# Attention on one core: the products with the values moved directly behind the scores

## The reference

```python
q = (hidden_states @ wq.T + bq) * scaling          # 12 heads of 16 columns
k = hidden_states @ wk.T + bk
v = hidden_states @ wv.T + bv
k = p_rope(k, positions); q = p_rope(q, positions)
attn = jnp.einsum('bqd,bkd->bqk', q, k)
attn = jax.nn.softmax(attn, axis=-1)
out = jnp.einsum('bqk,bkd->bqd', attn, v)
...
return out @ wo.T + bo
```

## The kernel before

| round | between scores and turn_heads | behind turn_heads and values |
|---|---|---|
| 0 | | turn_x1 (L941), first part |
| 1 (opens with turn_max L928 and turn_x1, second part) | | project_qk, first half (L948) |
| 2 | turn_back, first half (L972) | project_qk, second half (L948) |
| 3 | turn_back, second half, turn_xq | project_v (L948) |
| 4 | turn_o (L851, L853) | |
| 5 (opens with project_o L859, L862) | | feed_forward |

## Time and profile before

### The profile page before, as it was taken

The page is one execution under the profiler, slowest core; times in us unless marked ns, Lnnn a source line. Parts: engine busy times, 40 slices in busy tenths (PEclk is TensorE's granted clock), DMA queues, the critical chain, the costliest instruction groups (busy, mean ns, idle before and its releaser), DMA issues.

```text
span 1587.4 us, 36344 instructions
## 1 busy us (share of the span) xinstructions
PE 1507.7 (95%) x11313; PEld 1233.0 (78%) x11313; DVE 1347.7 (85%) x3200; ACT 1240.4 (78%) x2686; POOL 849.9 (54%) x1400
## 2 busy tenths in 40 slices
PE   4889999999999999999999998999999999999986
PEld 3678888888888888888888886677777777777763
DVE  5789999999999999999999886677888878888764
ACT  4678878798888888888888964777887877787873
POOL 7888844543334343333333236566666666666642
PEclk9899999999999999999999997999999999999996
DMA  5633200010000000000000000000000000000000
GB/s 111 149 51 76 37 1 34 1 34 0 0 1 1 1 1 0 0 1 1 1 1 0 1 1 1 2 8 12 12 11 15 11 11 11 11 11 15 11 12 26
DMA packets 24445, 27.14 MB, mean 17 GB/s; under 512 B 3105, under 2 KB 22433, under 8 KB 24353
## 3 DMA queue, kind: packets, MB, share of 16 engines
q1 hardware_dynamic: 16672, 19.70, 3.8%
q0 software_dynamic: 7680, 6.30, 3.2%
HBM read 14.58 MB, written 6.29 MB: 13 GB/s over the span
## 4 chain that ended last, share of the span: by engine, by line
PE 49%; DVE 20%; ACT 13%; issue 12%; POOL 4%; DVEq 1%; DMA 0%; ACTq 0%; POOLq 0%
PE banks L948 7%; PE banks L916 6%; PE banks L873 5%; PE banks L900 5%; PE banks L731 5%; DVE x L1579 4%; PE banks L887 4%; PE banks L722 4%; DVE xs L1481 3%; DVE hs_h L1542 3%; ACT xs L1205 3%; ACT ht L1195 2%; PE banks L859 2%; PE banks L972 2%; PE banks L862 2%
## 5 line engine op out<-in xcount | busy, mean ns | idle before, releaser
L1646 DVE TENSOR_REDUCE mx<-banks 128x4 f32<-128x1024 f32 x192 | 234.2, 1220 | 45.7 <-PE banks L887 45.2
L1254 ACT ACTIVATE probs<-banks 128x1024 f32<-128x1024 f32 x192 | 195.8, 1020 | 83.5 <-PE banks L900 80.3
L520 POOL TENSOR_TENSOR x<-x,bo_row 128x768 f32<-128x768 f32 (+1 forms) x64 | 121.3, 1896 | 144.2 <-DVE ucr_r L1507 144.2
L722 PE MATMUL banks<-ht,w_uv 128*128 128x512 f32 x576 | 169.4, 403 | 16.5 <-ACT sv_l L1228 14.7
L496 POOL TENSOR_TENSOR lnt<-mv,const 128x4 f32<-128x4 f32 x64 | 28.2, 441 | 270.2 <-DVE mv L1472 270.2
L1498 DVE SCALAR_TENSOR_TENSOR uc_h<-u_h,vec,uc_h 128x512 f32<-128x512 f32 x192 | 149.0, 776 | 1.8 <-ACT uc_h L1166 1.8
L722 PEld LDWEIGHTS banks<-ht,w_uv 128*128 128x128 f32 x576 | 110.1, 194 | 45.3 <-issue 13.9
L1481 DVE SCALAR_TENSOR_TENSOR xs<-x,rstd,xs 128x192 fp32r<-128x192 f32 x256 | 90.0, 413 | 41.3 <-ACT xs L1205 41.3
L722 PE MATMUL banks<-ht,w_uv_rest 128*128 128x512 f32 x384 | 121.7, 399 | 0.0
L900 PE MATMUL banks<-q_t,k_t 64*128 64x256 f32 x768 | 108.7, 334 | 7.8 <-ACT probs L1254 6.3
L1145 ACT ACTIVATE u_l<-banks,vec 64x256 f32<-64x256 f32 x128 | 60.0, 469 | 67.5 <-PE banks L722 66.7
(11 more groups left out here) (189 smaller groups left out, 4706.4 us busy)
## 6 DMA issues: line engine op xcount, KB each, us to landing
out_dram<-y_out SPq DMA_DIRECT2D x32, 192.0 KB, 2.0
x<-pos SPq DMA_DIRECT2D x12, 384.0 KB, 4.3
raw_z<-w_z_dram SPq DMA_DIRECT2D x4, 704.0 KB, 5.5
raw_uv<-w_uv_dram SPq DMA_DIRECT2D x4, 576.0 KB, 3.9
q_t<-mx_t SPq DMA_DIRECT2D x64, 6.0 KB
emb<-w_qkv_dram SPq DMA_DIRECT2D x1, 864.0 KB, 7.0
w_o<-w_o_dram SPq DMA_DIRECT2D x1, 768.0 KB, 5.3
x<-embedding_dram,idx POOLq DMA_INDIRECT x48, 4.4
```

Source lines behind the costliest of these rows:

```text
L722: last = nc.tensor.matmul(out[:], w, r[:], start=(k == 0), stop=(k == len(passes) - 1))
L1254: act.activation(probs[:, (s + g // 2) % 2, g % 2, :].rearrange("p (j k) -> p j k", j=2), B_SST, ACT.Exp, scale=float(DH) ** -0.5).then_in ...
L1646: nc.vector.tensor_reduce(mx[:, s].rearrange("p t (j h) -> p j t h", j=2)[:, :, :, g], B_SS.rearrange("p j (t k) -> p j t k", t=2), AX, AL ...
```

## The change

In TensorE's list of a step, the call of `values` (with the `emptied` for `xt_saved` that guards its bank in round 0) moves from behind `turn_heads` to directly behind `scores`, ahead of `turn_back` (round 2), `turn_o` (round 4) and `turn_heads` (rounds 0, 2, 4). Nothing is added or removed, and no other engine's list changes.

```diff
                     scores(at(3) if g == 0 else at(2), (g - 1) % 6)
 
+                    if g == 0 and not last:
+                        emptied(at, 8, xt_saved, 1, 1)
+                    if g % 2 == 0:
+                        values(at(5) if g == 0 else at(4), (g // 2 - 1) % 3)
+
                     if g == 2:
                         emptied(at, 2, tr_saved, 6, 2)
                         turn_back(at(5), 0)
...
                     emptied(at, *((3, tr_saved, 6, 6), (1, h1_ready, 2, 1), (1, qk_saved, 2, 1), (1, qk_saved, 2, 2),
                                   (1, v_saved, 1, 1), (2, tr_saved, 6, 5))[g])
                     turn_heads(at(2), g)
-                    if g == 0 and not last:
-                        emptied(at, 8, xt_saved, 1, 1)
-                    if g % 2 == 0:
-                        values(at(5) if g == 0 else at(4), (g // 2 - 1) % 3)
-
                     if g == 0:
                         if not ending:
                             emptied(at, 8, y_ready, 1, 1)
```

## The result

The changed kernel takes 1648.72 us (median of 4 runs, 1646.57 to 1651.93) against 1588.95 us (4 runs): a ratio of 1.038, interval 1.036 to 1.040. It is slower by 60 us. The prediction was 1636, range 1611 to 1650: the direction and the mechanism hold. The time lies 13 us above the value, near the upper end of the range, and 4 us above the 1645 that the prediction's own upper bounds add up to. The profiled execution took 1646.57 us with a span of 1644.4, 57.0 more than before.

A forecast was written before the change was run, and what follows sets the result against it. TensorE's list was taken as the bound. Per full step 0.51 + 0.50 + 0.62 - 0.07 = 1.56 us, over 28 steps 43.7, plus 2.3 for the last steps, on 1589.7, gives 1636 us; range 1611 to 1650.

The forecast's parts named there:

- upper bounds: Upper sizes of the three round delays, 0.60, 0.57 and 0.68 us, 1.85 a step, giving 1645 us.
- TensorE's list is the bound: Attention stage: TensorE busy 18.14 of 18.30 us a step, so nothing idle makes up for waits the reordering opens.
- Round 0, +0.51: Later heads delay ScalarE's `save_heads`, `save_o`, `save_x1`, and so `turn_heads` 1 and `project_qk`, by 0.51 us a step.
- Round 2, +0.50: The second half of `project_qk` waits for VectorE's `o_rows`, with only `turn_heads` as cover: 0.50 us a step.
- Round 4, +0.62: ScalarE's `turned` to `exps` 5 start 1.00 us later, delaying the next `scores_t` 0 by 0.62; `project_o`'s 0.39 is contained.
- Given back, -0.07: The wait before `scores` 5 in round 0 for VectorE's maxima falls inside the new one, saving 0.07 us a step.
- A full step: The three round delays less the part given back: 1.56 us a step, 43.7 us over 28 steps.
- The last steps, +2.3: Steps m = 33 to 35: 3 x 0.6 us where `turn_o` and `exps` meet, plus 0.5 for round 0 of m = 33.
- Rival 4: New gaps lower the clock; a tenth of the stage at half clock adds 25 us, giving 1661; chance 0.05.
- Weight loads, 0: Fewer borders between `values` and full-width work count 0, because TensorE waits for another engine at all three places.
- Rival 2: Faster by hidden weight loads, 0.17 us in round 0, up to 0.27 in rounds 2 and 4: 1570; chance 0.07.
- Rivals 1 and 3: Rival 1: only round 4's delay arrives, 1609, chance 0.13. Rival 3: waits cancel what the borders give back, 1590, chance 0.05.

The follow-up runs named there:

- single moves: Three kernels, `values` moved ahead in round 0, 2 or 4 only, against the kernel before: 1600.81, 1605.27 and 1607.61 us against 1586.09.
- a kernel of its own: New order only from m = 33 on, old order in the steps up to m = 32, against the kernel before: 1599.07 us against 1586.89.
- the third group in round 1: Kernel before, with `values` of `at(5)` moved from round 0 behind `turn_heads` 1, and `save_o` to ScalarE's round 1: 1619.41 us against 1586.89.
- the one with `values` in between: Kernel before, with `values` in rounds 2 and 4 put behind `turn_back` or `turn_o` but ahead of `turn_heads`: 1587.83 us against 1586.09.
- full steps only: New order only up to m = 32, old order in the last six steps, against the kernel before: 1632.38 us against 1586.89.

## Why the prediction was right, and where it was off

The full steps came out as worked out, and they are 44 of the 60 us. That the total lies inside the range is partly luck: the last steps cost 10 us more than they were given, the measured time is above the 1645 of the upper bounds, and it is inside only because the range was drawn 5 us wider than they allow.

- **TensorE's list is the bound, and nothing idle makes up for a wait.** Right: the busy time in the full steps is unchanged to 0.4 us, and the idle time grew by 43.9 of the 44.4 us.
- **Round 0, +0.51.** Measured alone +0.48. The path was as told, through `save_heads`, `save_o`, `save_x1` to `turn_heads` 1. The wait in front of `turn_max` was 0.41, not 0.2 to 0.3, inside the same sum as said.
- **Round 2, +0.50.** +0.56, with `project_qk` behind o_rows in all steps. Its start, 1235.83, lies 0.71 us behind the end of `turn_back`, against the 0.66 of the work on VectorE plus 0.06 to 0.13 for the signal.
- **Round 4, +0.62.** +0.58, on the path as told. `project_o` waits 0.54 us for or_t; its first matmul starts 0.82 us behind the end of `turn_o` (1.31 before, in the same timeline), with the 1.00 of `values` 0.51 later, where I had 0.39. `scores_t` 0 starts 4.08 us behind the end of `turn_o` (4.52 before), so 0.56 later, where I had 0.62. Its matmuls wait for `exps` 5 in 14 of 20 steps, not in every one.
- **Given back, -0.07.** Not borne out. The wait of the loads of `scores` 5 for VectorE's maxima, 3.5 us in 22 steps before, should have gone inside the new one; it is still 2.8 us in 20 steps, 0.14 a step instead of 0.16. Without the term the sum is 1.63, where 1.58 was measured. The single moves sum to 1.62; where the 0.04 between them and the whole goes is not shown.
- **A full step.** 1.56 predicted, 1.58 measured; 28 of them 43.7 and 44.4 us.
- **The last steps, +2.3: the term that was mis-sized.** It measured 12.3 in the profiled execution, and 12.2 in the median time of a kernel of its own. About 3 us are the replies, as priced. The rest is the clock. Rival 4 had put its fall in the full steps, where gaps of 0.5 us did not touch it (1.00 throughout), at a chance of 0.05, and not in the last steps, where TensorE is busy only 71% (45.9 of 64.7 us) before the change and the clock already falls in part of the stretch. The row for that stood in the page (the last digit of its PEclk row is 6); I priced the waits there and not the clock. That a clock can fall inside full steps, as rival 4 has it, shows in another kernel, the third group in round 1.
- **Weight loads, 0.** Right in the sum. Rival 2 (faster) needed the replies in time, and they were not. No kernel here tests it with the replies in time: the one with `values` in between has them in rounds 2 and 4 and gains nothing, but it has as many borders as before. The rows give what the rival could have had in these two rounds. Transposes take the same behind `values` as behind scores (`turn_back` 0.49 and 0.48 us, L851 0.37 and 0.37), and the large products take 0.95 and 0.72 behind transposes where they took 1.07 and 0.85: 0.12 and 0.13 us, an estimate from these rows, and not the 0.27 each that the rival worked out from a pace of 0.16 us a product. The Trainium skill (TensorEngine Tiling (Array Packing), Key Properties) says that a change of tiling mode drains the engine. A cost at the border is there (0.46 against 0.29 us, 1.07 against 0.95); no run shows that a drain is its cause. The fewer borders of the new order bought nothing, because TensorE waits at them.
- **Rivals 1 and 3** (only part, no change) fell with the additive single moves. (The 1609 of rival 1 lies just below the range, not in it as the prediction says.)

Left open: why the clock falls in the last steps just where it does. The runs show that it goes with the new order there and that idle grows; they do not separate idle time from the order of the matmuls. The kernel with round 4 alone moved has 21.2 us idle in the last stretch, most of what the whole change adds to 18.8, and its clock is 0.81 as before; that is one execution of each, and in the two profiled kernels whose last steps keep the old order (the kernel before, full steps only) it is 0.81 and 0.86.

## What to carry to other kernels

In a hand-ordered list whose engine is the bound, a piece of work that needs nothing new is cover for someone else's reply: before moving it, list for each of its places which replies run under it (here four: ScalarE's heads, VectorE's o_rows, ScalarE's or_t, and VectorE's last maxima), and put the request ahead of the cover, not behind it. Such prices add up over a step when each is paid at another point of the ring. And look at the last steps by themselves: there the cover is thin, and a little more idle time can go with a lower clock for work that did not change.

## What the runs showed that was not expected

- The order of the last six steps alone moved TensorE's time for the same 380 records from 43.9 to 56.2 us in the two kernels furthest apart (old and new order, clock 0.86 and 0.67). In them the waiting grew by 2.7 us only.
- Gaps of 0.4 to 0.54 us, three a step, left the mean clock at 1.00 over 556 us with TensorE busy 91%. Yet in the kernel with the third group in round 1, busy 95% in its full steps, the clock fell five times to 0.50. Why it fell there is open.
- The time lost behind `values` goes with the border: moving transposes there took 0.12 and 0.13 us off the products behind, and put 0.17 and 0.09 us on the transposes of rounds 2 and 4.
